# Even and odd partitions for the skewed copies, half the sums, and another hand-over to the routed stage, in an attention and mixture-of-experts kernel

## The reference, cut to what matters

```python
def block(x, ctx):                       # x [2, 2048, 512], ctx [2, 128, 512]
    x = x + xattn(layernorm(x), ctx)
    return x + ffn(layernorm(x))         # 4096 tokens
def xattn(xn, ctx):
    q, k, v = xn @ Wq + bq, ctx @ Wk + bk, ctx @ Wv + bv     # k, v padded to 2048
    corr = irfft(qf.real * kf.real - 1j * qf.imag * kf.imag)
    mean = corr.mean(heads and channels)                     # [2, 2048]
    weights, delay = top_k(mean, 15)
    return sum_k softmax(weights)_k * roll(v, delay_k) @ Wo + bo
def ffn(x):                              # 16 experts of 128, four to a token
    shared = (silu(x @ sg.T) * (x @ su.T)) @ sd.T            # 1024 hidden
    topk_idx, w = route(x)
    return shared + sum_e w_e * (silu(x @ gate_e) * (x @ up_e)) @ down_e
```

## Time and profile before

| | |
|---|---|
| three runs | 996.57, 997.05, 1002.86 us, median 997.05 us |
| profiled execution | 997.35 us |
| its span, first to last instruction | 995.5 us |
| PE busy | 983.8 us, 99% of the span |
| VectorE, POOL, ACT busy | 649.9, 478.1, 380.4 us |

### The profile page before, as it was taken

How to read it: one execution, slowest core, us unless ns; L and a number is a source line. 1 busy time by engine, 2 the same in 40 slices (tenths; PEclk the granted TensorE clock), 3 DMA queues, 4 the chain that set the end, 5 groups by cost and what they waited for, 6 DMA issues and landing times.

```text
span 995.5 us, 21034 instructions
## 1 busy us (share of the span) xinstructions
PE 983.8 (99%) x6750; PEld 601.3 (60%) x6750; DVE 649.9 (65%) x1506; ACT 380.4 (38%) x776; POOL 478.1 (48%) x540
## 2 busy tenths in 40 slices
PE   8999999999999999999999999999999999999998
PEld 7776644444444445557777777777777544444443
DVE  4977788874488898765555555555455375676765
ACT  3646454443445333324444444444444311111111
POOL 0725412131144577754445444454543376766662
PEclk9999999999999999999999999999999999999999
DMA  9735867868562721558889988889988579999675
GB/s 340 266 126 194 293 196 233 232 184 240 180 180 96 220 66 58 133 140 255 251 240 245 257 236 253 238 252 234 253 253 224 171 237 271 310 259 304 193 225 177
DMA packets 175484, 216.93 MB, mean 218 GB/s; under 512 B 101097, under 2 KB 112233, under 8 KB 174377
## 3 DMA queue, kind: packets, MB, share of 16 engines
q1 hardware_dynamic: 151640, 136.95, 46.6%
q0 software_dynamic: 23760, 78.79, 26.7%
HBM read 123.67 MB, written 69.22 MB: 194 GB/s over the span
## 4 chain that ended last, share of the span: by engine, by line
PE 84%; DVE 7%; DMA 4%; issue 2%; SPq 1%; ACT 1%; POOL 1%; another core or an unknown queue 0%; DVEq 0%; POOLq 0%; ACTq 0%
PE bank L1068 18%; PE bank L941 14%; PE bank L1131 14%; PE bank L1092 9%; PE bank L957 7%; PE bank L1144 7%; PE bank L1051 5%; PE bank L716 2%; PE bank L1082 2%; PE bank L793 1%; DMA arena<-in_x 1%; PE bank L696 1%; SPq L517 1%; PE bank L706 1%; DMA pt_dram<-arena 1%
## 5 line engine op out<-in xcount | busy, mean ns | idle before, releaser
L1068 PE MATMUL bank<-arena 128*128 x1716 | 211.1, 273 | 0.9 <-DVE arena L1608 0.9
L941 PE MATMUL bank<-arena 128*128 128x512 f16 x888 | 202.3, 379 | 0.5 <-DVE arena L1616 0.2
L1068 PEld LDWEIGHTS bank<-arena 128*128 128x128 f16 x1716 | 163.0, 98 | 26.5 <-issue 1.9
L2139 POOL DMA_INDIRECT arena<-y_dram,arena x128 | 137.0, 1071 | 76.8 <-issue 34.2
L2082 POOL DMA_INDIRECT arena<-xr_dram,arena x143 | 139.7, 977 | 58.4 <-issue 47.0
L941 PEld LDWEIGHTS bank<-arena 128*128 128x128 f16 x888 | 87.2, 99 | 101.0 <-DVE arena L1616 0.7
L1131 PE MATMUL bank<-arena 128*128 128x512 f16 x648 | 144.1, 379 | 0.0
L1092 PE MATMUL bank<-arena 128*128 x429 | 115.4, 378 | 0.8 <-ACT arena L1401 0.5
L1884 DVE SCALAR_TENSOR_TENSOR arena<-bank,arena 128x128 f32<-128x128 f32 x143 | 41.7, 292 | 109.7 <-ACT arena L1390 83.6
L1951 DVE SCALAR_TENSOR_TENSOR arena<-arena 128x512 f32<-128x512 f32 x128 | 95.4, 749 | 25.4 <-DMA arena<-y_dram,arena 19.8
L1131 PEld LDWEIGHTS bank<-arena 128*128 128x128 f16 x648 | 63.4, 98 | 76.5
(11 more groups left out here) (227 smaller groups left out, 1313.4 us busy)
## 6 DMA issues: line engine op xcount, KB each, us to landing
y_dram<-arena SPq DMA_DIRECT2D x143, 256.0 KB
arena<-in_x SPq DMA_DIRECT2D x8, 1024.0 KB, 12.5
xr_dram<-arena SPq DMA_DIRECT2D x16, 512.0 KB, 4.0
x_dram<-arena SPq DMA_DIRECT2D x8, 1024.0 KB, 5.8
arena<-in_gu_w SPq DMA_DIRECT2D x16, 512.0 KB, 3.5
out<-arena SPq DMA_DIRECT2D x32, 256.0 KB
arena<-x_dram SPq DMA_DIRECT2D x5, 1024.0 KB, 5.9
arena<-in_gu_w POOLq DMA_DIRECT2D x8, 512.0 KB, 4.8
```

Of the source, the lines that this page charges most:

```text
L941: last = mm(bank[half][:, :], (gu_hi_s, gu_lo_s)[wp][:, c, at:at + H], xt[:, xv * KC + kc, :], start=(n == 0), stop=(n == 3 * KC - 1))
L1068: last = mm(gate_up_bank(s, s)[:, 0:2 * H], rows[:, xv * KC + kc, :], only((gu_hi_r, gu_lo_r)[wp], e, slice(kc * 2 * H, (kc + 1) * 2 * H)) ...
L2139: pool.indirect_dma_start(out=ybuf[n % RING][:, e, :], out_offset=None, in_=y_dram[:, :], in_offset=bass.IndirectOffsetOnAxis(ap=row_of[:, ...
```

## The change

Even and odd partitions: the two skewed reads go to even partitions (the `skew_c` kind) and odd ones (the `skew_d` kind), rows 0 to 63 into a buffer "near" and rows 64 to 127 into "far". VectorE adds far to near in place (`fold_part`), and one f32 matmul with a column of 1 on even and -1 on odd partitions sums a tile: 32 in all. The fold has a semaphore, `skew_folded`. In batch 0 the number of transfers stays (a destination of every second partition, two halves in one transfer). In batch 1 each transfer is cut in two of half the size.

```diff
-SUM_AT = {(0, 0, 10): 1, (0, 0, 11): 2, **{(0, 1, n): i + 3 for i, n in enumerate((0, 1, 3, 4, 6, 7, 9, 10))},
-          (1, 0, 11): 0, **{(1, 1, n): n + 11 for n in range(NA - 11)}}
+SUM_AT = {**{(1, 0, n): n + 1 for n in range(10)}, (1, 0, 10): 0, (1, 0, 11): 11,
+          **{(1, 1, n): n + 12 for n in range(NA - 12)}}
...
-    c[:, C_ONES:C_ONES + 4] = [1, 1, 1, -1]
+    c[:, C_ONES:C_ONES + 4] = 1
+    c[1::2, C_ONES + 3] = -1
...
-                sp.dma_start(skew_c[0][:, max(lo - M, 0):hi - M], skewed(0, 2 * M - 1, PTW - 1, max(lo - M, 0), hi - M)
-                             ).then_inc(s_sk[0], 16)
-                sp.dma_start(skew_d[0][:, max(lo, M):hi], skewed(0, 1, PTW + 1, max(lo, M), hi)).then_inc(s_sk[0], 16)
+                sp.dma_start(skew_both[0:P:2, :, max(lo - M, 0):hi - M],
+                             skewed(0, 2 * M - 1, PTW - 1, max(lo - M, 0), hi - M)).then_inc(s_sk[0], 16)
+                sp.dma_start(skew_both[1:P:2, :, max(lo, M):hi], skewed(0, 1, PTW + 1, max(lo, M), hi)).then_inc(s_sk[0], 16)
...
+                    sp.dma_start(skew_both[1:P:2, :, 0:M], skewed(0, 1, PTW + 1, 0, M)).then_inc(s_sk2[0], 16)
+                else:
+                    for v, dst in enumerate((skew_near[1], skew_far[1])):
+                        sp.dma_start(dst[0:P:2, EARLY - M:L], skewed_half(1, 2 * M - 1, PTW - 1, EARLY - M, L, v)
+                                     ).then_inc(s_sk2[1], 16)
+                        sp.dma_start(dst[1:P:2, EARLY:L], skewed_half(1, 1, PTW + 1, EARLY, L, v)).then_inc(s_sk2[1], 16)
+                        sp.dma_start(dst[1:P:2, 0:M], skewed_half(1, 1, PTW + 1, 0, M, v)).then_inc(s_sk2[1], 16)
```

The sums on PE, and the order of batch 0:

```diff
-                mm(dst, skew_c[b][:, a * P:a * P + P], c_sb[:, C_ONES + 2 - SUM_W:C_ONES + 2], start=True, stop=False)
-                return mm(dst, skew_d[b][:, a * P:a * P + P], c_sb[:, C_ONES + 4 - SUM_W:C_ONES + 4], start=False, stop=True)
+                return mm(dst, skew_near[b][:, a * P:a * P + P], c_sb[:, C_ONES + 4 - SUM_W:C_ONES + 4],
+                          start=True, stop=True)
...
-            pe.wait_ge(s_sk[0], 32)
-            second_g_and_sum(1, (1, 2))
-            skewed_sum(0, 3)
+            second_g(1)
             turn_first(4)
-            for a in (4, 5, 6):
+            pe.wait_ge(s_fold, 1)
+            second_g_and_sum(2, (1, 2, 3, 4))
+            for a in (5, 6):
                 skewed_sum(0, a)
-            pe.wait_ge(s_sk[0], 64)
-            second_g_and_sum(2, (7, 8))
-            second_g_and_sum(3, (9, 10))
+            pe.wait_ge(s_fold, 2)
+            second_g_and_sum(3, (7, 8, 9, 10))
             pe.wait_ge(s_vw, 16)
             pe.wait_ge(s_pt_sb, 4)
-            pe.wait_ge(s_sk2[0], 48)
-            value_part_and_sum(0, (0, 11, 12))
-            summed = value_part_and_sum(1, (13, 14, 15))
+            value_part(0, bank[5], 0)
+            pe.wait_ge(s_fold, 3)
+            for a in (0, *range(11, NA)):
+                summed = skewed_sum(0, a)
             summed.then_inc(s_u, 1)
-            value_part(0, bank[5], 2)
+            value_part(0, bank[5], 1)
             pe.wait_ge(s_tables, 32)
             pe.wait_ge(s_mm_sb, 14)
             even_parts(0)
+            value_part(0, bank[5], 2)
+            mean_correlation(0)
             value_part(0, bank[5], 3)
-            mean_correlation(0)
```

In batch 1 all sixteen sums stand in chunk 1:

```diff
-                    if g == half == 0 and n == 10:
-                        pe.wait_ge(s_sk[1], 32)
+                    if g == 1 and half == 0 and n == 0:
+                        pe.wait_ge(s_fold, 4)
                         pe.wait_ge(s_pt_sb, 7)
-                    if g == 1 and half == 0 and n == 11:
-                        pe.wait_ge(s_sk2[1], 48)
+                    if g == 1 and half == 0 and n == 10:
+                        pe.wait_ge(s_fold, 5)
```

VectorE's folds and the router's constants:

```diff
+            def fold_part(b, lo, hi):
+
+                near = skew_near[b][:, lo:hi]
+                return V.tensor_tensor(near, near, skew_far[b][:, lo:hi], ALU.add)
+
+            def fold_late(b):
+
+                dve.wait_ge(s_sk2[b], 96 if b else 48)
+                fold_part(b, 0, M)
+                fold_part(b, EARLY - M, L).then_inc(s_fold, 1)
+
...
             normalise(4)
-            dve.wait_ge(s_misc, 64)
...
-            link.done(V.tensor_scalar(rt_hi, r3, WS, None, ALU.mult))
-            V.scalar_tensor_tensor(rt_lo, r3, WS, rt_hi, ALU.mult, ALU.subtract).then_inc(s_rt, 1)
-            V.tensor_copy(id16, c_sb[:, C_ID:C_ID + P]).then_inc(s_rt, 1)
...
+            for n, (lo, hi) in enumerate(STEPS[0]):
+                dve.wait_ge(s_sk[0], 32 * (n + 1))
+                fold_part(0, max(lo, M) if n == 0 else lo - M, hi - M).then_inc(s_fold, 1)
             V.memset(ones_row[0:1, :], 1.0)
-            dve.wait_ge(s_ids, 1)
-            V.tensor_scalar(token_id, token_int, -ID_MID, None, ALU.add)
-            V.memset(ones16, 1.0).then_inc(s_rt, 1)
             normalise(5)
+            fold_late(0)
...
             vo_low(0)
+            dve.wait_ge(s_misc, 65)
...
+            V.memset(chosen_after[:, 0:E], 0.0)
+            V.tensor_copy(places16, cr_sb[:, R_BLK:R_BLK + COLUMNS])
+            V.tensor_scalar(token_id, token_int, -ID_MID, None, ALU.add)
...
+                if g == 0:
+                    fold_late(1)
...
             x1_moments(1)
+            dve.wait_ge(s_sk[1], 64)
+            fold_part(1, M, EARLY - M).then_inc(s_fold, 1)
             shared_weights_lo(1)
```

POOL's additions of `bo` and its transfers:

```diff
-            for q in range(5):
+            for q in range(HALF - 1):
                 add_bo(q)
+            pool.wait_ge(s_ev_sb, 3)
+            add_bo(3)
+            add_bo(4, (0, 1))
             pool.wait_ge(s_mm, 18)
             pool.wait_ge(s_st[0], 16)
             for n in range(2):
                 shared_weights_in(n)
+            add_bo(4, (2, 3))
             add_bo(5)
             pool.wait_ge(s_lo0, TB)
             add_bo(6)
             pool.wait_ge(s_pte, 16)
             pool.wait_ge(s_u, 1)
             pool.wait_ge(s_mm, 28)
-            pool.dma_start(skew_c[1][:, 0:EARLY - M], skewed(1, 2 * M - 1, PTW - 1, 0, EARLY - M)).then_inc(s_sk[1], 16)
-            pool.dma_start(skew_d[1][:, M:EARLY], skewed(1, 1, PTW + 1, M, EARLY)).then_inc(s_sk[1], 16)
+            for v, dst in enumerate((skew_near[1], skew_far[1])):
+                pool.dma_start(dst[0:P:2, 0:EARLY - M], skewed_half(1, 2 * M - 1, PTW - 1, 0, EARLY - M, v)
+                               ).then_inc(s_sk[1], 16)
+                pool.dma_start(dst[1:P:2, M:EARLY], skewed_half(1, 1, PTW + 1, M, EARLY, v)).then_inc(s_sk[1], 16)
```

The cut, the counting and the end of the routed stage (`turn_rows(0)` comes into `shared_down(35)`; the last chunk ahead of the routed stage goes through its banks in the order 2, 0, 3, 1; counting runs in two chains; three matmuls of the first of `LAST` stand ahead of the last block's `down`):

```diff
-HOT = {26: (0, 4), 27: (4, 7), 28: (7, 11), 29: (11, 14), 30: (14, 18), 31: (18, 21), 32: (21, 25), 33: (25, 28), 34: (28, 32)}
+HOT = {26: (0, 4), 27: (4, 7), 28: (7, 10), 29: (10, 14), 30: (14, 18), 31: (18, 21), 32: (21, 25), 33: (25, 28), 34: (28, 32)}
...
+                    if g == AHEAD - 1 and i == 1:
+                        last.then_inc(s_cut, 1)
+                    if g == AHEAD - 2 and t == 1:
+                        pe.wait_ge(s_ss, AHEAD)
+                        turn_rows(0)
...
-            pe.wait_ge(s_ss, AHEAD)
-            turn_rows(0)
...
+                if s == BLOCKS:
+                    pe.wait_ge(s_txe, on_tensor(BLOCKS - 1) + 1)
+                    gate_up_at(LAST[0], (0, BEGUN))
                 if s:
                     down(s - 1, of[s - 1])
                 if s == BLOCKS - 1:
...
-                dve.wait_ge(s_sd, min(SH * (k + 1), AHEAD))
+                if k == CUT and order[0] == BANKS_FREE[0]:
+                    dve.wait_ge(s_cut, 1)
+                else:
+                    dve.wait_ge(s_sd, min(SH * (k + 1), AHEAD))
...
-            link.done(V.memset(counted, 0.0))
-            for e in range(E - 1):
-                link.done(V.scalar_tensor_tensor(counted, cr_sb[:, R_BLK:R_BLK + COLUMNS], last_blk[:, e:e + 1],
-                                                 counted, ALU.is_ge, ALU.add))
+            link.start(V.memset(counted, 0.0))
+            link.done(V.memset(counted_odd, 0.0))
+            for e in range(0, E - 1, 2):
+                for n, v in ((e, counted), (e + 1, counted_odd)):
+                    if n < E - 1:
+                        link.start(V.scalar_tensor_tensor(v, cr_sb[:, R_BLK:R_BLK + COLUMNS], last_blk[:, n:n + 1],
+                                                          v, ALU.is_ge, ALU.add))
+                link.wait()
...
+            order[0:4] = [0, 1, 3, 2]
```

More of the change, by code:

```diff
@@ L201, in build @@
         xg = view(o2, [4, 2 * D], F16)
-        counted = view(o1 + 8 * KB, [COLUMNS])
+        counted, counted_odd = view(o1 + 8 * KB, [COLUMNS]), view(o1 + 9 * KB, [COLUMNS])
         router_rows = view(o2 + 8 * KB, [2 * KC, BLK], F16)
@@ L320, in skewed, with skewed_half @@
         def skewed(b, start, pitch, first, end):
-            return bass.AP(pt_dram, b * P * PTW + start + first, [[pitch, P], [1, end - first]])
```

(52 more changed lines are left out.)

53 lines of the change are left out of this document (23 added, 30 removed).

## The result

The changed kernel takes 1003.74 us (median of six runs, 1002.85 to 1004.95) where the kernel before takes 996.41 (six runs). The ratio is 1.0062, interval 1.0044 to 1.008; on another chip it was 1.0082 (1.0055 to 1.011). So the change makes the kernel 6 to 8 us slower. 995.0 was forecast, with a range up to 999.0.

A forecast was written before the change was run, and what follows sets the result against it. PE was taken as the bound, busy 983.8 of 995.5 us at full clock. Terms -0.5 (sums), -0.86 (one-hot), -0.5 (cut) and -0.48 (end) sum to -2.3 against 997.35, giving 995.0 us; range 990.5 to 999.0.

The forecast's parts named there:

- Sums removed: Both batches: 16 sum matmuls fewer in each, 3.57 us in batch 0 and 3.6 in batch 1.
- The late fold: Batch 0: PE waits 1.2 us (bounds 1.0 and 2.8) ahead of six sums; batch 1: 0.3 to 0.6 us.
- rival (c): Reads into every second partition, or halves, land later; each us costs about 2 us, 2 us gives 999; chance 0.17.
- VectorE and POOL between the batches: Between batches: VectorE 1.7 us later among POOL's six additions, PE waits 1.2; router constants hidden in a gap.
- Ahead of chunk 1: Batch 1: 3.5 us of PE waiting, for SiLU of chunk 0 behind weights 2 and for VectorE's low parts.
- One-hot, cut, end: One-hot matmuls, counting cut and last down: gains of 0.86, 0.5 and 0.48 us.
- (b): Rival: the sums' gain stays, 9.5 us less, 988; with half of the sums' part kept 991.5; chance 0.13.

The follow-up runs named there:

- cover_b0: Changed kernel plus 12 f32 matmuls that nobody reads, ahead of batch 0's six late sums; ratio 1.0022 to the kernel before, 1001.98 us.
- pause_short: Kernel before plus one PE wait for VectorE's router constants, in batch 0's second g, a pause of 1.1 us; ratio 1.0076.
- cover_both: Changed kernel plus unread matmuls: 12 ahead of batch 0's late sums, ten ahead of the attention before chunk 1, six ahead of chunk 1; 1.0028, 1002.59 us.
- rest_only: Kernel before with only the one-hot table, the cut and three matmuls ahead of the last down; ratio 0.998, 997.27 us.
- both_covered: Changed kernel with four value parts ahead of batch 0's fold wait; batch 1: low parts 1 before large fold, SiLU 0 before weights 2, late sums last; 1.0062.
- reordered: Changed kernel with three value parts ahead of batch 0's fold wait, batch 1 rearranged, low parts of weights 2 behind chunk 0; ratio 1.0132.

## Why the prediction was wrong, point by point

- **Sums removed (7.2 us).** Right: 64 records fewer, sums of 0.14 and 0.23 us.
- **The late fold: 1.2 us forecast, 2.8 measured.** This term was mis-sized; 2.8 was its own upper bound. PE reached the six sums at 50.42, forecast 50.25. I took issue and landing as before. The rows of the last read and the fold after, against the earlier trace rows:

```profile
L486 SPq DMA_DIRECT2D arena<-pt_dram x1: 607/607/607, 47.6 to 47.6; - x1
...
DMA to landing us min/median/max: 4.5/4.5/4.5
```

```profile
52.13 1.03 DVE L1457 TENSOR_TENSOR arena<-arena 128x128 f32<-128x128 f32 x2 [3.98 <-DMA arena<-pt_dram]
...
87.05 2.99 DVE L1618 TENSOR_SCALAR arena<-arena 128x4 f32<-128x4 f32 x1
```

  Issuing one of these late reads takes SP 0.59 to 0.61 us, where it took 0.32 to 0.43. The third of them lands 3.6 to 4.6 us after its issue in the eight profiles with folds, and 3.0 to 4.3 in the eight without. So it lands at 52.1, not 50.3. The fold was 1.03 us, forecast 0.9. This is rival (c), about 2 us of later landing, which I had at 0.17; by its price the time would be 999, not 1004.
- **No fall of the clock was in the sum.** This is the step that failed. "Its granted clock is full (2.4 GHz) in all 40 slices, so the time is PE's work plus its waits" took the clock as given; it was full in a kernel whose PE paused nowhere between 25 and 370 us for more than 0.52 us. Each new wait was priced at its length. In batch 0 the fall cost 3.4 us in the changed kernel (cover_b0) and 6 to 10 in the kernel before (pause_short). No rival had it.
- **VectorE and POOL between the batches**: forecast a wait of 1.2, measured 1.86. The constants took 0.2 each in the gap, hidden, as forecast. The moments met POOL's six additions (82.60 to 90.00, where 85.0 was forecast for their end): one small instruction (L1618, the last row above) took 2.99 us, until 90.04, where it took 0.56.
- **Ahead of chunk 1**: 3.5 us forecast in two waits, 3.7 measured, on L1688 and L1354 as named. The mechanism was right: SiLU 0 hung on the transfer of weights 2, which POOL issued at 104.31 (98.67 before) and which took 8.4 us (8.1 before). The late fold, 0.3 to 0.6 in the sum, is not seen in the changed kernel, as PE, slow, came to it after it was ready; at full clock it takes 1.4 (cover_both).
- **One-hot, cut, end**: 1.8 forecast, 2.0 measured (rest_only). The waits at L974 and at the last `down` are gone. The cut came out by luck: its waits were to shrink by 0.5 us and grew.
- **The range** ended at 999.0. With the late fold's 2.8 the sum gives 996.6, with VectorE's 1.86 between the batches 997.3, with batch 0's fall 1000.7, a loss by itself. Another 2.2 comes from batch 1, which lost 3.4 us where 1.2 was forecast; `cover_both` shows that full clock there doesn't bring it back, so VectorE, the transfers and the late reads hold it. How much each of these takes is not separated. (The range's lower end was to be half of (b); that is 991.5 in the prediction's own sum, not 990.5, which changes nothing here.)

## What to carry to other kernels

Before a change that opens a new wait on a full PE, ask whether the clock survives it: a wait of 1 us cost 7 or more in most runs at one place, one of nearly 2 us only itself at another, and a full clock in the profile before says nothing of it. Look at the clock of every run and not of the profiled one alone. Halving PE's work helps only if what PE waits for next comes earlier too; put independent matmuls, even useless ones, ahead of such a wait. Price a transfer anew when its pattern changes, its issue on the queue too.

## What the runs showed of the hardware

- A pause of 1.1 us in PE's work, among f32 matmuls of 32 and 128 columns, is followed by 1.2 GHz for 13 us in the profile, and by a lower mean clock in eight runs of ten; one of 3.1 us by 20 us; one of 1.9 us at the f16 transposes by none, in nine profiles. In `both_covered` the clock fell behind pauses of at most 0.68 us. What sets these lengths is open.
- 12 f32 matmuls of 128 columns in the pause kept the clock at 2.4 GHz there in two profiles (`cover_b0`, `cover_both`).
- SP needed 0.6 us to issue a read into every second partition with two halves in a row (the late reads of batch 0), 0.32 to 0.43 for one into all partitions in the kernel before.
- A VectorE instruction with its input in on-chip memory can be held until GpSimd is done: L1618 took 2.99 us and ended with the last of GpSimd's six additions, and one that takes 0.68 us alone took 4.86 beside GpSimd's 4.08 (`reordered`).
